# RoPE partners in neighbouring tiles: rotation products removed, half-head rows, one store per query tile, 24 transfers per attention slot

## The reference, cut to what matters

```
x = x + attention_a(layernorm(x))     # latent keys and values, RoPE, 32 heads of 16
x = x + ffn(layernorm(x))             # dense + averaged LoRA
x = x + attention_b(layernorm(x))     # causal, ALiBi
x = x + ffn(layernorm(x))
```

```
q = (h @ Wq).reshape(B, S, 32, 16);  c = h @ Wc          # 64 latent channels
k = (c @ Wk).reshape(B, S, 32, 16);  v = (c @ Wv).reshape(B, S, 32, 16)
rotate_half(x) = concat([-x2, x1])                       # x1, x2: channels 0..7 and 8..15 of a head
q = q * cos + rotate_half(q) * sin;  k = k * cos + rotate_half(k) * sin
softmax(q k^T / 4) v, then @ Wo
```

## Time and profile before

| | |
|---|---|
| median of 3 runs | 1764.09 us (1759.22 to 1764.3) |
| the profiled execution | 1759.7 us |
| its span on the core | 1757.5 us |
| mean granted TensorE clock | 0.976 of full speed |
| PE busy | 1639.4 us, 93% of the span |
| DVE busy | 1402.2 us, 80% |
| ACT busy | 969.0 us, 55% |
| POOL busy | 214.1 us, 12% |
| DMA | 167.58 MB in 116801 packets |

### The profile page before, as it was taken

One profiled execution on the slowest core, in us unless ns is written; L12 is line 12 of the kernel. 1 busy time (PEld: TensorE's weight loads), 2 busy tenths in 40 slices (PEclk: granted clock), 3 DMA queues, 4 the chain that ended last, 5 costly groups with the idle time before them and its releaser, 6 DMA issues. The chain is left out here.

```text
span 1757.5 us, 32974 instructions
## 1 busy us (share of the span) xinstructions
PE 1639.4 (93%) x13040; PEld 847.7 (48%) x13040; DVE 1402.2 (80%) x2959; ACT 969.0 (55%) x1095; POOL 214.1 (12%) x272
## 2 busy tenths in 40 slices
PE   6998999999999999999999999999999999999888
PEld 3554333333333333333345777655455555554667
DVE  3766899999999999999548364568888888899675
ACT  3433277777777777777811112126666666667210
POOL 3332200000000000000022021021101000003331
PEclk9999699999999999999999999989999999999999
DMA  6765334333333333331140433763645464642211
GB/s 217 229 180 184 84 58 85 61 63 62 58 63 62 59 60 63 56 59 59 56 158 24 144 108 110 213 156 57 117 77 91 79 94 77 96 77 87 89 68 72
DMA packets 116801, 167.58 MB, mean 95 GB/s; under 512 B 20772, under 2 KB 58036, under 8 KB 116532
## 3 DMA queue, kind: packets, MB, share of 16 engines
q1 hardware_dynamic: 115176, 160.99, 40.4%
q0 software_dynamic: 1472, 4.49, 1.2%
HBM read 100.41 MB, written 64.50 MB: 94 GB/s over the span
## 5 line engine op out<-in xcount | busy, mean ns | idle before, releaser
L360 DVE TENSOR_REDUCE mxp<-ps_m 128x1 f32<-128x512 f32 x1280 | 798.6, 684 | 67.1 <-PE ps_m L326 62.6
L688 ACT ACTIVATE a_p<-a_ps_s 128x1024 f32<-128x1024 f32 x512 | 522.6, 1025 | 146.7 <-PE a_ps_s L609 128.9
L688 ACT ACTIVATE b_p<-b_ps_s 128x1024 f32<-128x1024 f32 (+1 forms) x320 | 294.9, 939 | 157.7 <-PE b_ps_s L609 154.3
L357 DVE CUSTOM_DVE_ANT_0 ps_m<-ps_m,b_masks 128x128 f32<-128x128 f32 (+3 forms) x512 | 239.8, 516 | 42.4 <-PE ps_m L326 37.6
L326 PE MATMUL ps_m<-slot_qk 62*128 62x512 f32 (+3 forms) x624 | 229.5, 449 | 12.3 <-DVE mxp L360 9.1
L326 PE MATMUL ps_m<-a_slot_qk 62*128 62x512 f32 x640 | 237.6, 449 | 0.8
L609 PE MATMUL a_ps_s<-a_slot_qk 64*128 64x512 f32 x640 | 231.7, 442 | 1.3
L633 PE MATMUL a_ps_o<-a_p,a_slot_v 128*32 128x256 f32 x2560 | 205.6, 390 | 9.9 <-ACT a_p L688 5.4
L609 PEld LDWEIGHTS a_ps_s<-a_slot_qk 64*128 64x128 f32 x640 | 96.2, 185 | 128.9 <-issue 122.7
L283 POOL CAST cparts<-negm 128x16 fp32r<-128x16 f32 x64 | 12.7, 198 | 1116.0 <-DVE negm L366 1116.0
L609 PE MATMUL a_ps_s<-slot_qk 64*128 64x512 f32 x384 | 134.9, 451 | 0.9 <-ACT a_p L688 0.3
(11 more groups left out here) (217 smaller groups left out, 2418.8 us busy)
## 6 DMA issues: line engine op xcount, KB each, us to landing
va_tokens<-w_o SPq DMA_DIRECT2D x16, 512.0 KB, 3.1
ka_parts<-pa_parts SPq DMA_DIRECT2D x16, 512.0 KB, 3.0
qa_parts<-pa_parts SPq DMA_DIRECT2D x32, 256.0 KB, 3.7
kb_parts<-slot_memory SPq DMA_DIRECT2D x16, 512.0 KB, 3.7
qb_parts<-slot_memory SPq DMA_DIRECT2D x32, 256.0 KB, 3.3
vb_tokens<-w_proj SPq DMA_DIRECT2D x16, 512.0 KB, 2.9
a_slot_qk<-qa_parts SPq DMA_DIRECT2D x60, 128.0 KB, 4.2
a_slot_qk<-ka_parts SPq DMA_DIRECT2D x48, 128.0 KB, 6.5
```

The lines of the kernel that those rows point to most:

```text
L357: dve.tensor_tensor_reduce(from_, from_, mask_of_query[:, CHUNK - keys:], 1.0, LOWEST, ALU.add, ALU.max, accum_out=to).then_inc(piece_take ...
L360: dve.tensor_reduce(to, from_, AX.X, ALU.max).then_inc(piece_taken, 1)
L688: act.activation(p_sb[:, (2 * u + pair) % NP, :, off:CHUNK], ps_s[:, 2 * pair:2 * pair + 2, off:CHUNK], ACT.Exp, scale=scale).then_inc(exp ...
```

## The change

In words: the columns of Wq and Wk are reordered on the host (`halves_apart`), so that of 16 heads the channels 0 to 7 come in one tile and the channels 8 to 15 in the next. The partner of a tile's channel then stands on the same partition of tile i ^ 1. The `rotated` products and the matrix `rot` are gone; DVE multiplies the neighbouring plain tile in SBUF by the sines and subtracts (even tiles) or adds (odd tiles). `copy_plain` waits for the roped form of both tiles of a pair before it overwrites a plain tile of the chunk before. The DRAM tensors of attention A are laid out with rows outermost and the two parts inside a row. A query tile is stored by one transfer, a key tile by one as before. A row of 16 channels of the slot is now in two runs of 8 rows, so a slot is loaded by 24 transfers of 8 rows. Attention B keeps its layout and its transfers.

The core of the diff:

```diff
     def load_q_row(self, e, r, tile, q_d, g, loaded):
         row = ROW_TILE * tile + DH * r
+        if self.runs == 2:
+            for a in range(2):
+                at, to = (2 * g + a) * GD, row + a * DH // 2
+                heads = q_d[at:at + GD, Q_PARTS[r], :].rearrange("(n e d) t -> e d n t", e=PAIR, d=DH // 2)
+                e.dma_start(self.q[to:to + DH // 2, :, :, :].rearrange("d a n t -> d (a n) t").bitcast(F32),
+                            heads[tile]).then_inc(loaded, 16)
+            return
...
     def load_k_row(self, e, r, tile, k_d, g, loaded):
         row = ROW_TILE * tile + DH * r
+        if self.runs == 2:
+            (b, m, own), n = (g // GPB, g % GPB * GD // (2 * P), g * GD // 2 % P), GD // 2
+            for a in range(2):
+                at, to = b * D + (2 * m + a) * P + own, row + a * DH // 2
+                heads = k_d[at:at + n, K_PARTS[r], :].rearrange("(n e d) t -> e d n t", e=PAIR, d=DH // 2)
+                e.dma_start(self.k[to:to + DH // 2, :, :].bitcast(F32), heads[tile]).then_inc(loaded, 16)
+            return
...
+def store_halves(sp, q_d, k_d, c, i, parts, sem):
+    b, half = c // 2, c % 2
+    m, a = divmod(i % KC, 2)
+    if i < KC:
+        row = b * D + (2 * m + a) * P
+        sp.dma_start(k_d[row:row + P, :, half * CHUNK:(half + 1) * CHUNK], parts.bitcast(F32)).then_inc(sem, 16)
+    else:
+        n = 2 * P // GD
+        row = (b * GPB + m * n) * 2 * GD
+        groups = q_d[row:row + n * 2 * GD, :, :].rearrange("(n a f r) w t -> a f n r (w t)", n=n, a=2, f=2)
+        sp.dma_start(groups[a, half], parts.bitcast(F32).rearrange("r w t -> r (w t)")).then_inc(sem, 16)
...
-        order += [("rotated", c, m) for m in range(KC)]
         order += turn_tasks[c + 1] if c + 1 < NC else []
-        order += [("q", c, 1), ("q", c, 2), ("rotated", c, KC), ("rotated", c, KC + 1), ("q", c, 3),
-                  ("rotated", c, KC + 2), ("rotated", c, KC + 3)]
+        order += [("q", c, m) for m in range(1, KC)]
...
                 if c:
-                    act.wait_ge(roped_ready, (c - 1) * PT + i + 1)
+                    act.wait_ge(roped_ready, (c - 1) * PT + (i | 1) + 1)
                 copy(plain(i), plain_task(c, i))
...
             def rope(c, i):
                 n = c * PT + i
-                task = ("rotated", c, i)
                 at = (c % 2) * CHUNK
-                banks.wait_full(dve, task)
+                banks.wait_drained(dve, plain_task(c, i ^ 1))
...
-                dve.tensor_tensor(by_sin[:, :], banks.out(task), sin[:, at:at + CHUNK],
-                                  ALU.mult).then_inc(banks.drain(task), 1)
-                banks.wait_drained(dve, task)
+                dve.tensor_tensor(by_sin[:, :], plain(i ^ 1), sin[:, at:at + CHUNK], ALU.mult).then_inc(sin_ready, 1)
+                dve.wait_ge(sin_ready, n + 1)
                 dve.wait_ge(cos_ready, n + 1)
                 dve.tensor_tensor(roped[:, n % MIX, :], by_cos[:, n % MIX, :], by_sin[:, :],
-                                  ALU.add).then_inc(roped_ready, 1)
+                                  ALU.add if i % 2 else ALU.subtract).then_inc(roped_ready, 1)
```

More of the change, by code:

```diff
@@ L66, in __init__ @@
         self.al = ALIBI_ROWS if biased else 0
+        self.runs = 1 if biased else 2
         self.zero_row = SROWS + self.al
@@ L149, in wait_loaded @@
         own_rows = PAIR * (3 if self.al else 1)
-        e.wait_ge(self.all_loaded, 16 * (PAIR * (len(Q_PARTS) + len(K_PARTS)) + 1 + own_rows))
+        e.wait_ge(self.all_loaded, 16 * (PAIR * self.runs * (len(Q_PARTS) + len(K_PARTS)) + 1 + own_rows))
 class Early:
@@ L208, in attention_plan @@
     MXB = EARLY_BANKS
-    K_LOAD = 16 * PAIR * (len(K_PARTS) + (1 if causal else 0))
-    LOAD = 16 * PAIR * len(Q_PARTS) + K_LOAD
+    K_LOAD = 16 * PAIR * (ready[0].runs * len(K_PARTS) + (1 if causal else 0))
+    LOAD = 16 * PAIR * ready[0].runs * len(Q_PARTS) + K_LOAD
     SETS = 16 * PAIR * (2 if causal else 1)
@@ L983, in _ @@
                     sp.dma_start(w["v"][:, :], env["Wv"]).then_inc(attn_loaded, 16)
-                    for t, name in ((cos, "cos"), (sin, "sin"), (rot, "rot")):
+                    for t, name in ((cos, "cos"), (sin, "sin")):
                         sp.dma_start(t[:, :], env[name]).then_inc(table_loaded, 16)
@@ L1049, in _ @@
             pe.wait_ge(w_split, 2)
-            pe.wait_ge(table_loaded, 48)
             for c in range(NC):
-                def rotated(i):
-                    task = ("rotated", c, i)
[L1054 to L1058, removed]
                 x_parts = [lambda kc: xnt[:, c % 2, kc, :], lambda kc: xnt_low[:, c % 2, kc, :]]
@@ L1084, in _ @@
                               start=True, stop=True).then_inc(banks.fill(task), 1)
-                for i in range(KC):
-                    rotated(i)
                 if c + 1 < NC:
@@ L1099, in _ @@
                 maxima(3, 4)
-                rotated(KC)
-                rotated(KC + 1)
                 query(3, lambda half: maxima(4 + half, 5 + half))
[L1103 to L1106, removed]
+                maxima(6, early.pieces // PAIR)
         @block.scalar
@@ L1122, in high @@
                 if n >= PARTS:
-                    act.wait_ge(parts_stored[n % PARTS], stored_counts(n // PARTS))
+                    act.wait_ge(parts_stored[n % PARTS], early.stores.counts(n // PARTS))
                 act.wait_ge(roped_ready, n + 1)
@@ L1738, in build @@
     }
-    for a in "ab":
-        env[f"q{a}_d"] = nc.dram_tensor(f"q{a}_parts", [2, 2 * B * D, CHUNK], F32).ap()
-        env[f"k{a}_d"] = nc.dram_tensor(f"k{a}_parts", [2, B * D, S], F32).ap()
+    for a, (q_shape, k_shape) in (("a", ([2 * B * D, 2, CHUNK], [B * D, 2, S])), ("b", ([2, 2 * B * D, CHUNK], [2, B * D, S]))):
+        env[f"q{a}_d"] = nc.dram_tensor(f"q{a}_parts", q_shape, F32).ap()
+        env[f"k{a}_d"] = nc.dram_tensor(f"k{a}_parts", k_shape, F32).ap()
         env[f"v{a}_d"] = nc.dram_tensor(f"v{a}_tokens", [B * P, 8 * H * VW], F32).ap()
@@ L1800, in build @@
                 sb("cparts", [P, PAIR, SHIFT_ROWS, 4 * GH // PAIR], F32R), sb("cturned", [SHIFT_ROWS * 4 * GH, P]))
-        early_a = Early(nc, ctx, "a", False, consts, [first], ps_m, rows, Stores(nc, ctx, "a"), 24)
-        early_b = Early(nc, ctx, "b", True, consts, [first_b, second_b], ps_m, rows, Stores(nc, ctx, "b"), 48)
+        early_a = Early(nc, ctx, "a", False, consts, [first], ps_m, rows, Stores(nc, ctx, "a", 1, 1), 24)
+        early_b = Early(nc, ctx, "b", True, consts, [first_b, second_b], ps_m, rows, Stores(nc, ctx, "b", 1, P // GD), 48)
         with ExitStack() as weights:
@@ L1838, in shape_constants @@
     freqs = np.arange(S, dtype=np.float32)[:, None] * inv_freq
[L1839 to L1845, removed]
+    angle = freqs.T
     row, column = (np.arange(P) % ROW_TILE)[:, None], np.arange(P)[None, :]
@@ L1856, in shape_constants @@
     return {
-        "cos": np.tile(np.cos(angle), (P // DH, 1)).astype(np.float32),
-        "sin": np.tile(np.sin(angle), (P // DH, 1)).astype(np.float32),
-        "rot": rot,
+        "cos": np.tile(np.cos(angle), (2 * P // DH, 1)).astype(np.float32),
+        "sin": np.tile(np.sin(angle), (2 * P // DH, 1)).astype(np.float32),
         "ident": np.eye(P, dtype=np.float32),
@@ L1878 @@
     host = {name: np.ascontiguousarray(inputs[name]) for name in NAMES}
+    for name in ("L0_attn_a_Wq", "L0_attn_a_Wk"):
+        host[name] = halves_apart(host[name])
     host.update(shape_constants())
```

24 lines of the change are left out of this document (13 added, 11 removed).

## The result

The changed kernel took 1825.52 us (median of 4 runs, 1816.44 to 1833.34) against 1762.37 before (median of 4 runs, one more than in the table of before): a ratio of 1.0347, 95% interval 1.0311 to 1.0382, so 55 to 67 us slower. The forecast was 1820, in a range of 1768 to 1885. The profiled execution took 1824.86 us with a span of 1822.6, 65.1 more than before.

A forecast was written before the change was run, and what follows sets the result against it. It took project_a for a chain of waits, with value stores queued behind query stores. Late stores +48, POOL's issues +3 and attention steps +3 made +54 on 1759.7, 1814, forecast as 1820; range 1768 to 1885.

The forecast's parts named there:

- Engines follow the outermost dimension: DMA transfers use the largest engine count up to 16 dividing both sides' outermost sizes: 4 for query stores.
- 8-row loads: Slot loads on 8 engines: a slot takes 20.2 us in place of 10.1, no longer hidden in project_a's chunk 2.
- 5.1 us per query store: A query store of 512 KB in project_a takes 5.1 us on four engines, in place of 2.5.
- half-rate rival: In project_a, engines sharing ports run at half rate: stores up to 10.2 us, +71, about 1885; chance 0.12.
- The chain: In project_a, slow query stores delay value stores, ACT's value copies and finally POOL's clears: +48 us.
- V1, V2, V3: When ACT's value waits end in chunks 1 to 3 of project_a: forecast 84.7, 128.0 and 183 us.
- the clears: POOL's clears behind project_a, once the last stores land: forecast to start at 231 in place of 182.76.
- A us of store time is worth 14: In project_a, 14 or 15 query stores lie on the chain from 84.7 on, so each us counts 14.
- POOL's issues: Six more issues on POOL ahead of PE's turn at the attention's opening, 0.53 us each: +3.0 us.
- Steps of the attention: In 13 attention steps shift rows land later behind slower loads, 0 to 1 us each: +3, bounds 0 and 13.
- Rotated products: project_a without 32 products of 0.46 us: chunk 0's query store issues at 66.7 not 67.88, a later stretch 25.3 not 26.1.

The follow-up runs named there:

- loads16: As both16, but each query tile stored by four transfers with DRAM side 4 x 8 x 1024 (4 engines): 1804.04 us, ratio 1.0229.
- four_stores: The changed kernel with each query tile stored by four transfers of 32 rows x 1024: 1768.46 us, ratio 1.0025.
- both16: The changed kernel with DRAM rows laid out so query stores have 16 as outermost dimension and loads 16 rows, 18 per slot: 1759.23 us, ratio 0.9975.
- after_v_four: The changed kernel with four value buffers in place of two: 1800.37 us, ratio 1.0205.
- parts_first: The changed kernel with POOL's first shift rows made ahead of its wait for the stores, the clears and the key issues: 1813.34 us, ratio 1.0297.
- one_store: The kernel before, rotated products kept, with one 128-row store per query tile of attention A: 1760.47 us, ratio 0.9981.
- v_four: both16 with four value buffers in place of two: 1751.33 us, ratio 0.9926.
- one_store_v_four: one_store (rotated products kept) with four value buffers in place of two: 1752.69 us, ratio 0.9933.

## Why the prediction was right

- **Engines follow the outermost dimension.** Right, and shown: shares of 0.25 to 0.27 for the 4 x 32 x 1024 stores, 0.48 for 8-row loads, and the pair loads16 (0.24) and four_stores (0.96), with both16 as the third. This is what the Trainium skill says in "DMA: Bandwidth & Descriptors", section "Why a DMA increments its semaphore by 16 and not by 1". That all query stores use the same four engines was assumed: 103 GB/s over 16 us in which four of them are queued fits it, since transfers on other engines would have run side by side. So does after_v_four, where ACT's waits in chunk 3 end at 160.36, 165.67 and 170.64: the stores land about 5 us apart.
- **5.1 us per query store.** Right: 103 GB/s. The half-rate rival is out. Two engines that would share ports by the Trainium skill ("SBUF — State Buffer", section "Door 1: The DMA port swizzle (why [64,N] ≈ [32,N])") still had 25.8 GB/s each. That each engine takes one run of 32 rows is read from the shape of the transfer and shown by no view. No run varied the rows that the four engines read, so why they don't hinder each other stays open.
- **The chain.** The links are right: parts_first and after_v_four show two of them, POOL's order and the value buffers. V1, V2, V3 were forecast at 84.7, 128.0 and 183 and measured at 86.50, 131.28 and 180.41, the clears at 231 and 231.51. That the clears fit within 0.5 us is partly luck, for the parts miss by more and cancel: V1 is 1.8 us late, V1 to V2 took 1.5 more than reckoned, V2 to V3 5.9 less, and V3 to the clears 3.1 more.
- **8-row loads.** The size is wrong. They were priced at 10 us in chunk 2. From V2 to V3 the changed kernel takes 49.1 us and loads16 46.2; with fast stores it is 33.8 in four_stores (106.81 to 140.59) and 31.8 in both16 (108.89 to 140.69). So they cost 2 to 3 us there. That the clears of loads16 lie 9.9 us earlier agrees with the 10 by chance.
- **A us of store time is worth 14.** Too small: 3.1 us less per tile moved the clears by 52.4, 17 for each. The prediction counts 14 or 15 stores from 84.7 on, but its own sum has eleven behind that point and three ahead of it.
- **POOL's issues.** +3.0 forecast, 3.65 measured (0.57 each, not 0.53).
- **Steps of the attention.** +3 forecast with bounds 0 and 13, 5.2 measured. The place was right, the spread and the size were not: the loss is 1.1 us in one step and 3.4 in another, under 0.4 in each of the others. I priced the waits, not the clock that falls behind them.
- **Rotated products.** The reckoning took off 1.2 us in chunk 0 and 0.8 between V1 and V2, 2.0 in all. It rests on a misread row: the trace before has 64 records of L1057, two for each of the 32 products, so six records in 2.74 us are three products of 0.9 us, and not six of 0.46. The stage shows 3.6 us (both16 against one_store) and 2.1 (v_four against one_store_v_four). Collisions are there: DVE's sine product took up to 1.77 us where before it never passed 0.69. In the timeline of chunk 1, beside POOL's cosine products (67.23 to 73.58):

```profile
67.61 1.44 DVE L1239 TENSOR_TENSOR w_q<-w_proj,pa_sin 128x512 f32<-128x512 f32 x1 [0.28 <-ACT w_proj L1127]
69.09 1.65 DVE L1242 TENSOR_TENSOR w_q<-o_memory,w_q 128x512 f32<-128x512 f32 x1
```

- **Not forecast:** 1.6 us of low clock behind the opening, which the kernels without rotated products lose and those with them don't. The sum was 54 against 59.2 at the end of attention A. The medians lie 63.2 us apart. That 1820 missed 1825.52 by no more than 5.5 is helped by two things outside the sum: 2 us added in rounding up, and a median of before that stood at 1764.09 and came down to 1762.37 with the fourth run.

## What to carry to other kernels

Before two transfers are merged or one is split, write down the outermost dimension of both sides and the engines it allows: four issues of 32 x 1024 beat one of 4 x 32 x 1024 by 57 us here, and a layout that puts 16 heads outermost gave the same merge without the loss. Price a slow store by what queues behind it in the same engines and by how many buffers stand between that and the compute: two more value buffers were worth 8 us with fast stores and 25 with slow ones. A removed operation on an engine that waits anyway can be worth almost nothing, however many of it there are: the 32 products gained 2 to 4 us in their stage, and 2 of them went back at a lower clock behind it. When a forecast fits, compare its intermediate points too, as V1 to V3 here: the total can fit while a term of it is three times too large.

## What the hardware showed that was not expected

- Transfers of 32 rows by 4 KB, issued one behind the other, stored at 262 GB/s (share 0.96), more than the 212 of the 64-row stores before.
- A PE wait of 1.26 us for a transfer was followed by some 6 us at a granted clock of 0.53, with PE busy throughout, and cost the step 3.4 us.
- After the opening of the attention, at 0.50 in all of these kernels, the clock rose in the first 5 us of scores where the rotated products were kept (0.87 before, 0.78 in one_store_v_four) and only in the next five where they were gone (0.50, then 0.70 in both16 and 0.69 in v_four). That took back 2 us of a stage gain of 5.6, and all of the 2.1 us between the two kernels with four value buffers.
